# State-space stage of a two-layer block: the state product in three products of split factors

## The reference, cut to what matters

```python
scores = einsum('bcihn,bcjhn->bcijh', Cc, Bc) * Ldec * dtc[:, :, None, :, :]
y_intra = einsum('bcijh,bcjhp->bcihp', scores, xc)
states = einsum('bcjh,bcjhn,bcjhp->bchpn', dtc * dlast, Bc, xc)   # the state product
# scan over chunks: state <- decay of the chunk * state + states
y_inter = einsum('bcihn,bchpn->bcihp', Cc * exp(cum)[..., None], prev)
y = y_intra + y_inter + D * x          # then gated by silu(gate), normed by group, projected
```

## Time and profile before

| | |
|---|---|
| median of 3 runs | 2262.8 us (2262.0 to 2267.0) |
| the profiled execution | 2265.07 us, of which 2263.1 us are the span from first to last instruction |
| mean granted clock of TensorE in it | 0.975 of full speed |
| busy in the span: TensorE, VectorE, ScalarE, GpSimd | 2116.1, 1469.1, 1374.9, 885.5 us |
| state-space stage | from about 640 to 1877 us |
| one group of the loop | 157 us |

### The profile page before, as it was taken

The page is one execution under the profiler, slowest core; times in us unless marked ns, Lnnn a source line. Parts: engine busy times, 40 slices in busy tenths (PEclk is TensorE's granted clock), DMA queues, the critical chain, the costliest instruction groups (busy, mean ns, idle before and its releaser), DMA issues. The chain is left out here.

```text
span 2263.1 us, 37073 instructions
## 1 busy us (share of the span) xinstructions
PE 2116.1 (94%) x12040; PEld 1566.3 (69%) x12040; DVE 1469.1 (65%) x1813; ACT 1374.9 (61%) x2396; POOL 885.5 (39%) x758
## 2 busy tenths in 40 slices
PE   6889999898699999999999999999999977999998
PEld 5634444476587777777777777777777755888886
DVE  4446666274468777778778687677778664555555
ACT  2145555433378888888788788788788762333222
POOL 0011111130147666667667566575766670000000
PEclk9989999998899999999999999999999997999999
DMA  4422222232335545445454455455455546444462
GB/s 132 157 79 69 77 72 62 75 125 60 93 115 174 160 154 157 151 146 164 148 163 155 126 179 158 132 159 159 140 167 158 166 165 244 142 141 141 141 213 75
DMA packets 184055, 310.81 MB, mean 137 GB/s; under 512 B 20512, under 2 KB 96800, under 8 KB 183744
## 3 DMA queue, kind: packets, MB, share of 16 engines
q1 hardware_dynamic: 183872, 308.53, 43.6%
HBM read 252.52 MB, written 55.68 MB: 136 GB/s over the span
## 5 line engine op out<-in xcount | busy, mean ns | idle before, releaser
L145 PE MATMUL ssm_pp<-xhi,ssm_lo 128*128 128x512 f32 x1192 | 482.9, 405 | 34.4 <-issue 15.2
L147 PE MATMUL ssm_pp<-xhi,ssm_hi 128*128 128x512 f32 x1192 | 469.8, 394 | 0.0
L146 PE MATMUL ssm_pp<-xlo,ssm_hi 128*128 128x512 f32 x1192 | 469.5, 394 | 0.0
L1413 ACT ACTIVATE ssm_sct<-ssm_cumb,ssm_gpar 128x128 f32<-128x128 f32 x1024 | 313.0, 390 | 57.3 <-DMA ssm_cumb<-dt_sums 49.7
L1508 DVE SCALAR_TENSOR_TENSOR ssm_xc<-ssm_pp,vectors,ssm_xc 128x1022 f32<-128x1022 f32 (+2 forms) x192 | 245.3, 1278 | 125.4 <-ACT ssm_xc L1374 110.5
L137 POOL TENSOR_TENSOR ssm_lo<-ssm_raw,ssm_hi 128x512 fp32r<-128x512 f32 x149 | 263.1, 1770 | 111.0 <-ACT ssm_hi L126 110.9
L145 PEld LDWEIGHTS ssm_pp<-xhi,ssm_lo 128*128 128x128 f32 x1192 | 226.4, 190 | 102.1 <-issue 34.3
L147 PEld LDWEIGHTS ssm_pp<-xhi,ssm_hi 128*128 128x128 f32 x1192 | 226.4, 190 | 49.0
L146 PEld LDWEIGHTS ssm_pp<-xlo,ssm_hi 128*128 128x128 f32 x1192 | 226.5, 190 | 43.7
L1543 DVE TENSOR_TENSOR ssm_sct<-ssm_sct,ssm_cbm 128x1024 f32<-128x1024 f32 x128 | 228.3, 1783 | 34.4 <-ACT ssm_sct L1420 19.2
L1674 POOL TENSOR_TENSOR ssm_go<-ssm_t,ssm_gt 128x512 f32<-128x512 f32 x128 | 164.6, 1286 | 177.0 <-DVE ssm_t L1579 112.8
(11 more groups left out here) (210 smaller groups left out, 4028.3 us busy)
## 6 DMA issues: line engine op xcount, KB each, us to landing
ssm_cumb<-dt_sums SPq DMA_DIRECT2D x96, 1024.0 KB, 6.3
ssm_raw<-w SPq DMA_DIRECT2D x149, 256.0 KB, 2.7
gated<-ssm_go SPq DMA_DIRECT2D x128, 256.0 KB, 4.9
out_graw<-gated SPq DMA_DIRECT2D x64, 512.0 KB, 4.2
out_raw<-w SPq DMA_DIRECT2D x65, 256.0 KB, 2.7
ssm_cumb<-dt_sums SPq DMA_DIRECT2D x32, 512.0 KB, 4.5
ffn_raw<-w SPq DMA_DIRECT2D x37, 256.0 KB, 2.8
stk_qs<-qk_parts SPq DMA_DIRECT2D x96, 64.0 KB, 2.2
```

What stands on the lines that cost most here:

```text
L145: pe.matmul(out, wlo, xhi, start=start, stop=False)
L146: pe.matmul(out, whi, xlo, start=False, stop=False)
L147: return pe.matmul(out, whi, xhi, start=False, stop=stop)
L1413: i = act.activation(sct[:, s % 2, h, :], cumb[:, s % 2, 0, h, :], ACT.Relu, scale=-1.0, bias=gpar[:, unit, 0, s % NTOK, h:h + 1])
```

## The change

The state product is formed like the projections. B is split when it is copied: ScalarE writes `bt_hi`, and VectorE, behind the scores of step 0, writes `bt_lo` (`b_low`); the slot of "turn B" is free only after that, and the first state product of a group waits for it. The weighed chunk is split too: at the top of a step with a state product ScalarE copies `xw` to `xw_hi` (`weighed_high`), and at the top of the step GpSimd subtracts (`weighed_low`) to get `xw_lo`. The state product is three matmuls, and waits for `xw_lo`. `xw` has one buffer now, and so have its two parts, which live in the tiles of the weight split of dt, no longer used by then. So the weighing waits for the last subtraction in place of the state product, and the copy waits for the last state product. The sums for the norm of the last group (`rms`) move into the tile of the causal mask, and SyncE waits for the last mask before it fills them.

```diff
         pre_done, pre_out = sem("pre_done"), sem("pre_out")
+        bt_hi_done, xw_hi_done, xw_lo_done = map(sem, "bt_hi_done xw_hi_done xw_lo_done".split())
         rms_in, rms_sum, rms_std, rms_inv, rms_out = map(sem, "rms_in rms_sum rms_std rms_inv rms_out".split())
...
         cc = sb("cc", [P, T])
-        btok = sb("btok", [P, NTOK, N])
+        sbr = lambda n, s: ctx.enter_context(nc.sbuf_tensor(f"ssm_{n}", s, F32R))
+        bt_hi, bt_lo = sbr("bt_hi", [P, NTOK, N]), sbr("bt_lo", [P, NTOK, N])
         cbm = sb("cbm", [P, NTOK, CS])
...
         xp = sb("xp", [P, 2, CU * P])
-        xw = sb("xw", [P, 2, CU * P])
+        xw = sb("xw", [P, CU * P])
+        xw_hi, xw_lo = dt_feed.hi[:, 0, :], dt_feed.lo[:, 0, :]
         state = sb("state", [P, 2, CU * P])
...
         na = sb("na", [P, 1])
-        rms = sb("rms", [P, 2, (G - 1) * T // P])
+        rms = c.causal[:, 0:2 * ((G - 1) * T // P)].rearrange("p (u n) -> p u n", u=2)
         rms_eps = sb("rms_eps", [P, 1])
...
                         sp.wait_ge(var_out, 2 * (G - 1) * B * 16)
+                        sp.wait_ge(cb_done, G)
                         for unit in range(2):
...
                 if ch < NC - 1:
-                    pe.wait_ge(xw_done, g * NCA + (carried(s) + 1))
+                    pe.wait_ge(xw_lo_done, g * NCA + (carried(s) + 1))
                     after(pe, state_done, g * NCA + carried(s))
...
                         after(pe, var_done, var_before(g, s))
-                    pe.matmul(p_state[:], btok[:, t, :], xw[:, s % 2, :], start=True, stop=True
-                              ).then_inc(states_done, 1)
+                    product(pe, p_state[:], bt_hi[:, t, :], bt_lo[:, t, :], xw_hi, xw_lo, True, True
+                            ).then_inc(states_done, 1)
                 elif summed and s % NTOK < NC:
...
                 e = ENTRIES.index("turn B")
-                act.activation(btok[:].rearrange("p c n -> p (c n)"), slot(e), ACT.Copy).then_inc(bt_done, 1)
+                act.activation(bt_hi[:].rearrange("p c n -> p (c n)"), slot(e), ACT.Copy).then_inc(bt_hi_done, 1)
                 act.wait_ge(x_done, g * NCV + 2)
...
                 act.activation(cc[:], bc[:, 1, :], ACT.Copy).then_inc(c_copied, 1)
+
+            def weighed_high(g, s):
+                if s % NC < NC - 1:
+                    act.wait_ge(xw_done, g * NCA + (carried(s) + 1))
+                    after(act, states_done, g * NCA + carried(s))
+                    act.activation(xw_hi, xw[:], ACT.Copy).then_inc(xw_hi_done, 1)
 
...
                         copy_b_c(g)
+                    weighed_high(g, s)
                     for e in AT[s - 1][-1:] if s else ():
...
 
+            def b_low(g):
+                dve.wait_ge(bt_hi_done, g + 1)
+                e = ENTRIES.index("turn B")
+                dve.tensor_tensor(bt_lo[:].rearrange("p c n -> p (c n)"), slot(e),
+                                  bt_hi[:].rearrange("p c n -> p (c n)").bitcast(F32), ALU.subtract).then_inc(bt_done, 1)
+
             def scaled(g, s):
...
                     scores(g, s)
+                    if s == 0:
+                        b_low(g)
                     if before(g, s, 1):
...
                     pool.wait_ge(xp_done, n + 1)
-                    after(pool, states_done, g * NCA + carried(s - 1))
-                    pool.tensor_tensor(by_head(xw[:, s % 2, :]), by_head(xp[:, s % 2, :]), heads(2, s), ALU.mult
+                    after(pool, xw_lo_done, g * NCA + carried(s))
+                    pool.tensor_tensor(by_head(xw[:]), by_head(xp[:, s % 2, :]), heads(2, s), ALU.mult
                                        ).then_inc(xw_done, 1)
+
+            def weighed_low(g, s):
+                if s % NC < NC - 1:
+                    pool.wait_ge(xw_hi_done, g * NCA + (carried(s) + 1))
+                    pool.tensor_tensor(xw_lo, xw[:], xw_hi.bitcast(F32), ALU.subtract).then_inc(xw_lo_done, 1)
 
...
                 for s in range(NS):
+                    weighed_low(g, s)
                     for e in AT[s - 1] if s else ():
...
                         if is_tile(e) and exists(r, last):

```

## The result

| | before | after |
|---|---|---|
| median of 4 runs each, on one chip | 2262.4 us (2261.2 to 2267.0) | 2307.7 us (2306.8 to 2309.5) |
| ratio, 95% interval | | 1.0197 (1.018 to 1.0215) |
| span of the profiled execution | 2263.1 us | 2305.4 us |
| mean granted clock of TensorE | 0.975 | 0.969 |

Slower, as forecast, but by 45 us where 9 were forecast, and outside the range (2248 to 2288).

A forecast was written before the change was run, and what follows sets the result against it. TensorE was taken as the bound, busy 152.49 of 156.88 us a group. Seven groups at +1.1 us (7.7) plus 1.1 for the last gave 8.8 us on 2262.8: 2272 us, range 2248 to 2288.

The forecast's parts named there:

- SP, "I add nothing": SyncE's weight loads wait for splits up to 2.3 us later, sums' loads queue behind; ScalarE itself 1.8 us later: 0 added.
- The sign that the prediction had named for a wrong reading of GpSimd's queue: TensorE's idle time ending on the subtraction in the first seven groups would show GpSimd's queue was misread; no size given.
- Steps 12 to 15: Group's end: ScalarE's queue of 29.3 us frees the bank for the transposes of B late, +0.97 us a group.
- Steps 4 to 6 and 8 to 10: Late copies on ScalarE eat the product's gains of 0.8 and 1.6 us: about 0 left, then +0.1 at step 11's tile.
- The last group: Steps 12 to 14 have no tile to hide copy and subtraction: 2.5 us lost, 1.4 gained, so +1.1 us.
- TensorE's part: Each state product takes 0.69 us instead of 0.95: 0.26 us less, 25 us less TensorE work over 96 products.
- Steps 0 to 2: VectorE ends last, step 3's tile still starts at 1130.36; three products' 0.8 us are lost, so 0.
- The race: In steps 1 and 2 GpSimd's subtraction asks 0.2 us before VectorE's scores, so VectorE's chain stays as long.
- The first rival: In steps 1, 2 and 9 VectorE's scores go before GpSimd's subtraction, 1.1 us less each: 2251 us, chance 0.20.
- nothing waits: Copy and subtraction hide everywhere in the kernel and 25 us come off: 2238 us, chance 0.06.
- The third rival: TensorE's clock falls after longer waits before the tiles of steps 3 and 15, some 22 us: 2294 us, chance 0.12.
- The low part of B: VectorE's one extra op a group, 1.23 us behind step 0's scores: costed at nothing, 10 us without that cover.

The follow-up runs named there:

- the sums first: Changed kernel with SyncE issuing the load of the cumulated sums ahead of the weight loads in each step: 2284.7 us.
- The copy alone: Changed kernel without GpSimd's subtraction of the weighed chunk, the high part standing in for the low part; ScalarE's copies stay: 2298.2 us.
- the subtraction alone: Changed kernel without ScalarE's copy of the weighed chunk; GpSimd does a subtraction of the same form that waits only for its own weighing: 2268.8 us.
- the three matmuls alone: Kernel before with the state product as three matmuls on parts written once in the shorter form, without copy, subtraction or added wait: 2255.9 us.
- both edits: Changed kernel with the sums' load ahead of the weight loads and, in a group's last step, the gate's silu ahead of the exponential: 2263.9 us.
- the silu is first: Changed kernel with both edits, and the gate's silu ahead of the exponential in steps 3 and 10 too: 2257.4 us.
- SyncE's edit: Kernel before with only the load of the cumulated sums issued ahead of the weight loads on SyncE: 2260.0 us.

## Why the prediction was wrong, point by point

**Direction right, size wrong.** The sum was 8.8 us; the measured 45 are four losses, 51 us together, less 5.5 us gained elsewhere.

1. **SP, "I add nothing": the step that failed.** The prediction saw that the loads of the sums stand behind the weight loads, and that these wait for the weight splits. It set this at nothing because ScalarE would get to the decays 1.8 us later itself. It looked at step 2, where a single split waits, and at no other of the twelve steps. In step 4 the subtraction waits 3.00 us for a copy that starts 2.3 us behind its weighing, since ScalarE is still at a gate; two splits stand behind the subtraction, and the loads of the sums behind the pair of weight loads. Nor was ScalarE 1.8 us late by itself there: with the sums first its decays of chunk 5 start 11.3 us behind the transposes of chunk 4 in the loop's groups, as early as they ever do there in the kernel before. With the sums ahead 23 us came back, and 17 with the subtraction behind the splits; forecast 0. The sign that the prediction had named for a wrong reading of GpSimd's queue is there: TensorE waits 0.80 us for the subtraction in steps 5 and 6.
2. **Steps 12 to 15: right mechanism, mis-sized term.** The turn of B does wait for the gate's silu. The sum had +0.97 us a group, the trace 2.22. Predicted was a ScalarE queue of 29.3 us from the first copy; it is 30.4 (1080.91 to 1111.27). The missing 1.0 is the idle time of the second copy, at 1092.80, whose weighing took 2.03 us beside VectorE's work: a wait that the sum counted in steps 4 to 6 but not here. And TensorE reached the turn 0.2 us sooner. The stretch costs 17.3 us where 7 were forecast.
3. **Steps 4 to 6 and 8 to 10: the chain was right, its end wasn't.** The late copies were seen (+0.9 and +1.5), with the gain of the product as what they eat, and about 0 left. The copy alone has +5.8 us in the stretch from 6 to 8: where the sums are late as well, the scores that start late end the convolution late, and the next tile waits for that (2.07 us above). With the sums first the stretch loses nothing (-2.8). In steps 10 and 11 the forecast was +0.1 for the first tile of step 11. That tile does wait for the gate's silu, 0.42 us, and the one before it 0.86 us for a convolution; the stretch from 10 to 12 costs 11.3 us over the groups.
4. **The last group: right chain, mis-sized term.** The chain weighing, copy, subtraction stands in front of the products as described: TensorE waits 5.38 us in step 12 where it was 3.38. TensorE after the change:

```profile
1882.57 0.80 PE L145 MATMUL ssm_pstate<-dtw_hi,ssm_bt_lo 128*128 128x512 f32 x1 [5.38 <-POOL dtw_lo L1676]
```

   The end costs 6.2 us; taken were 2.5, between 2 and 6. The next product waits too, 3.58 us, where the kernel before waited for nothing. The copy alone costs 4.1 us there and the subtraction alone 4.5.

**TensorE's part was mis-sized**: 0.26 us for a product came from the pitch inside a long row of split matmuls. With its first and last pitch it is 0.07 us for the product itself (0.95 to 0.88) and 0.16 with the way from the transposes: the three matmuls alone gain 7 us, where 0.26 us for the six products of a group that no wait swallows gives 12.

**What held.** Steps 0 to 2 gained nothing and the tile of step 3 waits 1.33 us for the convolution (about 1.5 was said). The race went as said, by GpSimd and VectorE of step 1 after the change:

```profile
1126.43 1.50 POOL L1676 TENSOR_TENSOR dtw_lo<-ssm_xw,dtw_hi 128x512 fp32r<-128x512 f32 x1 [0.74 <-ACT dtw_hi L1413]
...
1126.69 2.32 DVE L1554 TENSOR_TENSOR ssm_sct<-ssm_sct,ssm_cbm 128x1024 f32<-128x1024 f32 x1
```

The subtraction asks 0.26 us ahead of the scores (0.2 was said), and the scores take 2.32 us where 1.21 is their time alone. The Trainium skill's page "SBUF — State Buffer", section "SBUF: two separate sides", states such a lock for the pair; the trace agrees. The first rival (the scores win) therefore had no case, and "nothing waits" neither. The third rival, a fallen clock before the tiles of steps 3 and 15, didn't come: behind the stalls of 1.33 and 0.80 us there the matmuls follow each other by 0.23 us. What cost clock was the edge, where the stall was long already. The low part of B shows no cost, as said: with both edits the stretch from 0 to 1 is at +0.4.

**Open**: what of the 11.3 us from 10 to 12 is left (+3.7) once the silu is first. The idle time there ends on VectorE's convolution, ahead of the tile of step 10, and it goes with the subtraction: from chunk 10 to 11 the subtraction alone has +5.5, the copy alone +1.6, the three matmuls alone +0.4. From 11 to 12, where the tile waits for the silu, it is the copy: +4.4 alone, the subtraction -0.8. By which way the subtraction makes that convolution late isn't shown. No order was tried against the 6 us of the last group's end.

## What to carry to other kernels

Price an instruction that waits by every queue it heads: walk each step from it to the next engine (here GpSimd to SyncE to ScalarE to VectorE to TensorE), since the stall shows 30 us behind its cause and under another name. Before splitting one product, price it with its first and last pitch and with the copies that feed it: here 7 us were to be had, and 52 us of copies and waits (2307.7 against 2255.9) stood against them until two instructions were reordered; with both in their new places it is 8 (2263.9). Work added to an engine that is 80% busy takes the room that hid other waits there: look first for loads that were late already and cost nothing, and for what else stands behind the new work.

## What the hardware showed that I had not expected

- Between two forms of matmul the pitch is longer here: 0.31 us into the split ones and 0.33 out of them, where it is 0.23 to 0.24 within (timeline above). So a short row of split matmuls is worth less than its share of a long one: 0.88 us for three, not 0.69.
- A GpSimd operation can get shorter as another is added: the state's decay took 1866 ns on average before and 1064 after, the weight split's low part 1770 and 1518. In step 1 above the subtraction and the split fall beside VectorE's scores, which end at 1129.01, and the state's decay starts behind that, at 1130.13, and takes 1.07 us. GpSimd's busy time in a group grew by 3.1 us for 18 us of new work.
- The first tile behind the loop's edge takes between 5.6 and 8.5 us in one and the same kernel, with the granted clock that goes with it (both edits; stretch, length, busy PE, PEld, DVE, ACT, POOL, clock):

```profile
943.36:948.94 5.58, 5.58 (x25) 4.56 (x26) 2.81 (x6) 4.87 (x13) 4.88 (x5) 1.00 0.58 198
1099.22:1107.67 8.45, 8.45 (x24) 6.61 (x25) 2.58 (x6) 4.52 (x12) 4.94 (x5) 0.64 0.57 189
```

The first is at the full 2.4 GHz throughout, the second for the larger part at 1.2. The stalls ahead of them are 3.03 and 3.19 us: 0.16 us apart, and the tiles 2.9 us. So a stretch that holds this edge can differ by some us with no cause in the edit (in the kernel before with SyncE's edit it is 2.1 us longer over the groups, while each other stretch agrees within 1 us), and it is compared over all groups, not in one.
